# A fused vision-attention-experts kernel: another order for the last steps of its token stage

## The reference, cut to what matters

```python
h = _L0_tok_ref(x, ...)                       # (4, 256, 192)
h = jnp.concatenate([h, txt], axis=1)         # 12 tiles of 128 rows
h = h + _L0_attn_ref(_layernorm(h, axis=-1), ...)
h = h + _L0_ffn_ref(_layernorm(h, axis=-1), ...)

# in _L0_attn_ref: 12 heads of 16, hs = the normed rows
q = hs @ Wq.T + bq
v = hs @ Wv.T + bv
q = jnp.swapaxes(q.reshape(s, b, NH, HD), 0, 1).reshape(NH, BN, HD)
q = q / jnp.maximum(jnp.linalg.norm(q, axis=2, keepdims=True), 1e-12)
v = jnp.swapaxes(v.reshape(s, b, NH, HD), 0, 1).reshape(BN, NH, HD)
```

## Time and profile before

| what | value |
|---|---|
| three runs | 743.79, 733.47, 739.37 us, median 739.37 |
| the profiled execution's own time | 738.72 us |
| its span, first to last instruction | 737.0 us (1.7 us lie around it) |
| mean granted clock of TensorE | 0.94 of 2.4 GHz |
| busy, share of the span | PE 86%, DVE 58%, ACT 52%, POOL 48% |

### The profile page before, as it was taken

The page is one execution under the profiler, slowest core; times in us unless marked ns, Lnnn a source line. Parts: engine busy times, 40 slices in busy tenths (PEclk is TensorE's granted clock), DMA queues, the critical chain, the costliest instruction groups (busy, mean ns, idle before and its releaser), DMA issues.

```text
span 737.0 us, 17256 instructions
## 1 busy us (share of the span) xinstructions
PE 634.6 (86%) x4926; PEld 428.6 (58%) x4927; DVE 429.7 (58%) x1430; ACT 379.7 (52%) x721; POOL 356.2 (48%) x401
## 2 busy tenths in 40 slices
PE   5888899888884999899999998549999999999970
PEld 5775786677641223222222223438999999999970
DVE  0347767676664235555555554537777777777750
ACT  0323438343312999988999898014344344344330
POOL 3112233222232125555555545514777787787781
PEclk9999999999985999999999999559999999999995
DMA  8999999400014426545555231059898999999834
GB/s 325 409 353 303 328 313 333 164 1 1 23 53 112 68 115 192 154 143 140 150 153 150 58 71 58 37 191 300 214 249 230 229 252 235 232 255 231 228 64 77
DMA packets 78192, 132.61 MB, mean 180 GB/s; under 512 B 36859, under 2 KB 62892, under 8 KB 76876
## 3 DMA queue, kind: packets, MB, share of 16 engines
q1 hardware_dynamic: 64892, 116.79, 50.7%
q0 software_dynamic: 11712, 14.19, 11.7%
q10 hardware_dynamic: 1552, 1.18, 0.5%
HBM read 105.53 MB, written 58.42 MB: 222 GB/s over the span
## 4 chain that ended last, share of the span: by engine, by line
PE 58%; DVE 10%; ACT 9%; DMA 8%; issue 6%; POOL 6%; another core or an unknown queue 1%; SPq 1%; ACTq 0%; DVEq 0%; POOLq 0%
PE ps L864 11%; PE ps L1015 9%; PE ps L851 9%; PE ps L1044 6%; PE ps L1025 5%; DMA odd_sum<-mid 4%; ACT big L1137 3%; ACT mid L1137 3%; PE ps L701 2%; PE ps L710 2%; POOL rstd L492 2%; DVE stat L1225 1%; DVE mid L1233 1%; PE ps L786 1%; DMA out<-mid 1%
## 5 line engine op out<-in xcount | busy, mean ns | idle before, releaser
L1137 ACT ACTIVATE mid<-ps 128x1536 f32<-128x1536 f32 x108 | 152.6, 1457 | 27.1 <-PE ps L851 26.3
L627 POOL TENSOR_TENSOR mid<-mid 128x384 f32<-128x384 f32 x63 | 81.2, 1289 | 53.2 <-DVE mid L1563 23.8
L851 PE MATMUL ps<-mid 52*128 52x512 f16 x432 | 88.0, 396 | 20.7 <-ACT big L1137 8.5
L1015 PE MATMUL ps<-mid,big 128*128 128x128 f32 x756 | 99.3, 282 | 0.3 <-ACT mid L1163 0.3
L1015 PEld LDWEIGHTS ps<-mid,big 128*128 128x128 f32 x756 | 91.5, 194 | 4.6 <-ACT mid L1163 0.5
L1554 DVE TENSOR_SCALAR mid<-ps,big 128x128 f32<-128x128 f32 x189 | 54.6, 344 | 62.0 <-PE ps L1025 34.7
L864 PE MATMUL ps<-mid 128*32 128x384 f32 x864 | 87.3, 507 | 0.0
L1170 ACT ACTIVATE mid<-mid 128x384 f32<-128x384 f32 x63 | 32.9, 522 | 88.4 <-DVE mid L1554 74.6
L1044 PE MATMUL ps<-big,mid 128*128 x378 | 71.0, 332 | 4.6 <-POOL mid L627 3.9
L851 PEld LDWEIGHTS ps<-mid 52*128 52x128 f16 x432 | 17.1, 95 | 85.8 <-ACT mid L1137 46.1
L1044 PEld LDWEIGHTS ps<-big,mid 128*128 128x128 f32 x378 | 60.1, 190 | 9.8 <-issue 9.6
(11 more groups left out here) (224 smaller groups left out, 1108.6 us busy)
## 6 DMA issues: line engine op xcount, KB each, us to landing
big<-w_cat SPq DMA_DIRECT2D x63, 576.0 KB
expert_in<-expert_in SPq DMA_DIRECT2D x16, 1774.5 KB, 48.4
big<-expert_in SPq DMA_DIRECT2D x63, 136.5 KB
w_cat<-w_a SPq DMA_DIRECT2D x4, 1536.0 KB, 7.6
big<-w SPq DMA_DIRECT2D x2, 2304.0 KB, 8.9
big<-patches SPq DMA_DIRECT2D x8, 512.0 KB, 8.8
big<-patches SPq DMA_DIRECT2D x2, 2048.0 KB, 21.9
w_cat<-w_b SPq DMA_DIRECT2D x2, 1536.0 KB, 7.5
```

The source lines that it names most:

```text
L627: nc.gpsimd.tensor_tensor(actv[r], prod[r], sig[r], ALU.mult).then_inc(actv_ready, 1)
L851: last = nc.tensor.matmul(SETS[kb % 2][:, c * 512:(c + 1) * 512], keysT[n_par][row:row + STK, kb * P:(kb + 1) * P], qrysT[n_par][row:row + ...
L1015: last = nc.tensor.matmul(banks[half][:, c * P:(c + 1) * P], w1_t[q][:, half * FF + c * P:half * FF + (c + 1) * P], xtT[r][:, 0:P], start= ...
L1137: nc.scalar.activation(probs[kb % 4], SETS[kb % 2], ACT.Exp, scale=0.5).then_inc(probs_ready, 1)
```

## The change

The last 18 steps of the list are put in an order written out by hand, `CLOSE`. The order before, from the same step on, was: PP text(8,11), PT0, H1, T2, D2(3), PP0, PT1, H2, T3, S0, PP1, PT2, H3, S1, PP2, PT3, S2, PP3. ACT copies the projections instead of DVE, so PP takes banks 2 and 3. The norms get two sets of small tiles, `h_nrm` and `hnT` two pairs, and in some steps the statistics of a norm are taken in one step and the scaling (`norm_apply`, `head_norm`) is put later. POOL's five memsets of the stacks move from S0 to the PT step of text tiles (2, 5), with two more memsets and a wait. SP sends head 0's stacks before the v of images 2 and 3, with b1 and b2 right behind the stacks, and gathers the quarters of images 2 and 3 together at the end.

```diff
+CLOSE = [("PT", 0, 0), ("PP", 0, None), ("D2", 1, 3), ("H", 0, 1), ("T", LAYERS, 2), ("PP", 0, 0), ("T", LAYERS, 3),
+         ("PT", 0, 1), ("H", 0, 2), ("H", 0, 3), ("S0", 0, 0), ("PP", 0, 1), ("PT", 0, 2), ("PT", 0, 3),
+         ("S1", 0, 0), ("S2", 0, 0), ("PP", 0, 2), ("PP", 0, 3)]
...
+    begin = names.index(("PP", 0, None), names.index(("PP", 0, None)) + 1)
+    named = dict(zip(names[begin:], order[begin:]))
+    order[begin:] = [named[name] for name in CLOSE]
...
-ACC_JOBS = {"conv": 2, "A": 2, "K": 1, "C": 2, "D2": 2, "H": 2, "PP": 2}
-ACT_JOBS = {"T": 1, "A": 2, "D1": 2, "PT": 1}
+ACC_JOBS = {"conv": 2, "A": 2, "K": 1, "C": 2, "D2": 2, "H": 2}
+ACT_JOBS = {"T": 1, "A": 2, "D1": 2, "PT": 1, "PP": 2}
...
                 if stage == "S2":
                     sp.wait_ge(acc_taken, weights_read)
                     stacks(0, 0)
+                    sp.dma_start(b1_rows, w1_b[CB:CB + 1, :].rearrange("o (k c) -> (o k) c", c=P)).then_inc(b1_in, 16)
+                    sp.dma_start(b2_sb, b2).then_inc(b2_in, 16)
                 if stage == "PP":
-                    sp.wait_ge(acc_taken, jobs)
+                    sp.wait_ge(act_taken, acts)
...
-                    if b is not None:
+                    for image in {None: (), NB - 1: (NB - 2, NB - 1), NB - 2: ()}.get(b, (b,)):
 
                         sp.wait_ge(v_out, 16 * sent)
...
             sp.wait_ge(v_in, 16 * NB)
-            sp.dma_start(b1_rows, w1_b[CB:CB + 1, :].rearrange("o (k c) -> (o k) c", c=P)).then_inc(b1_in, 16)
-            sp.dma_start(b2_sb, b2).then_inc(b2_in, 16)
...
+                if stage == "PT" and tiles[0] == 2:
+
+                    pool.wait_ge(acc_taken, ctx_jobs)
                     nc.gpsimd.memset(key_both[:, :, :, 50:52], -0.5).then_inc(consts_ready, 1)
...
+                    for i, t in enumerate(hnT[1]):
+                        pool.wait_ge(consts_ready, NCONST + 5 + i)
+                        nc.gpsimd.memset(t[CB:CB + 1, P:2 * P], 1.0).then_inc(consts_ready, 1)
+                    pool.wait_ge(consts_ready, NCONST + 7)
+                if stage == "S0":
                     norm_root(0)
...
+                if stage == "PP":
+                    for t in tiles:
+                        src = act_job()
+                        nc.scalar.activation(qv[:, t, :], src[:, 0:2 * C], ACT.Identity).then_inc(act_taken, 1)
...
+            def head_norm(count, tiles):
+
+                if count >= 2:
+                    dve.wait_ge(act_ready, pt_jobs[count - 2])
+                norm_apply(head_lns[count], [h_res[:, t, :] for t in tiles], h_nrm[count % 2])
...
-                    image_norm(b)
+                    if (stage, l, b) == ("D2", LAYERS - 1, NB - 1):
+                        norm_stats2(image_rows(x_res, b))
+                        late_norm = lns[0] - 1
+                    else:
+                        image_norm(b)
...
                 if stage in ("H", "N"):
-                    if pt_job:
-                        dve.wait_ge(act_ready, pt_job)
-                    layer_norm([h_res[:, t, :] for t in tiles], h_nrm)
+                    norm_stats2([h_res[:, t, :] for t in tiles])
+                    head_lns.append(lns[0] - 1)
+                    if stage == "N" or b == 0:
+                        head_norm(len(head_lns) - 1, tiles)
+                    if (stage, b) == ("H", 1):
+                        norm_apply(late_norm, image_rows(x_res, NB - 1), image_rows(x_nrm, NB - 1))
+                    if (stage, b) == ("H", 3):
+                        head_norm(len(head_lns) - 2, rest)
+                    rest = tiles
...
                 if stage == "PT":
-                    pt_job = acts
-                if stage == "PP":
-                    for t in tiles:
-                        src = acc_job()
-                        nc.vector.tensor_copy(qv[:, t, :], src[:, 0:2 * C]).then_inc(acc_taken, 1)
+                    if b in (1, 3):
+                        head_norm(len(head_lns) - 1, tiles)
+                    pt_jobs.append(acts)
                 if stage == "S0":
-                    dve.wait_ge(acc_taken, acc[0])
+                    dve.wait_ge(act_taken, acts)
                     prep_squares(0)
```

More of the change, by code:

```diff
@@ L74, in schedule @@
     order[1:3] = [order[2], order[1]]
+    names = [job[:3] for job in order]
+    begin = names.index(("PP", 0, None), names.index(("PP", 0, None)) + 1)
+    named = dict(zip(names[begin:], order[begin:]))
+    order[begin:] = [named[name] for name in CLOSE]
     return order
 NORMS = ("conv", "C", "D2", "H", "N")
-ACC_JOBS = {"conv": 2, "A": 2, "K": 1, "C": 2, "D2": 2, "H": 2, "PP": 2}
-ACT_JOBS = {"T": 1, "A": 2, "D1": 2, "PT": 1}
-TOK_ACC = sum(ACC_JOBS.get(_s, 0) for _s, *_ in schedule())
+ACC_JOBS = {"conv": 2, "A": 2, "K": 1, "C": 2, "D2": 2, "H": 2}
+ACT_JOBS = {"T": 1, "A": 2, "D1": 2, "PT": 1, "PP": 2}
+TOK_ACC, TOK_ACT = [sum(_jobs.get(_s, 0) for _s, *_ in schedule()) for _jobs in (ACC_JOBS, ACT_JOBS)]
 def fusion_kernel(nc, patches, conv_w, cols, rows, qkv_w, out_w, ff1_w, ff2_w, head_w, txt,
@@ L157, in fusion_kernel @@
         wqvb_sb = mid[0:CB + 1, 6528:6912]
-        hnT_both = mid[:, 6912:7424].rearrange("p (s n) -> p s n", s=2)
-        hnT = [hnT_both[:, s, :] for s in range(2)]
-        h_nrm = [mid[:, 7424 + 192 * i:7616 + 192 * i] for i in range(2)]
+        hnT_both = [t.rearrange("p (s n) -> p s n", s=2) for t in (mid[:, 6912:7424], hnT_more)]
+        hnT = [[both[:, s, :] for s in range(2)] for both in hnT_both]
+        h_nrm = [[mid[:, base + 192 * i:base + 192 + 192 * i] for i in range(2)] for base in (7424, 8752)]
         rows_sb = mid[:, 7808:7808 + 5 * D]
@@ L204, in fusion_kernel @@
         nhalf = sb("nhalf", [P, NT])
[L206 to L209, removed]
+        stat, mv = [[sb(f"{name}{i}", [P, 2, n]) for i in range(2)] for name, n in (("stat", 6), ("mv", 2))]
+        vps, rstd = [[sb(f"{name}{i}", [P, 2]) for i in range(2)] for name in ("vps", "rstd")]
         sq = sb("sq", [P, C])
@@ L381, in _ @@
             v_rows = v_dram.rearrange("(t p) c -> p t c", p=P)
-            jobs = sent = 0
+            jobs = acts = sent = 0
             for stage, _, b, tiles in schedule():
                 jobs += ACC_JOBS.get(stage, 0)
+                acts += ACT_JOBS.get(stage, 0)
                 if stage == "C":
@@ L473, in _ @@
                                allow_small_or_imprecise_dtypes=True).then_inc(consts_ready, 1)
-            for i, dst in enumerate((hnT[0], hnT[1], tT)):
+            for i, dst in enumerate((*hnT[0], tT)):
                 pool.wait_ge(consts_ready, NCONST - 3 + i)
@@ L497, in norm_root @@
                 nc.gpsimd.tensor_tensor(nrm[:], ss[:], phalf[:, 0:NH], ALU.pow).then_inc(nrm_ready, 1)
-            norms, qs = 0, 0
-            for stage, l, b, _ in schedule():
-                if stage == "S0":
+            norms, qs, jobs = 0, 0, 0
+            for stage, l, b, tiles in schedule():
+                jobs += ACC_JOBS.get(stage, 0)
+                if stage == "K":
+                    ctx_jobs = jobs
+                if stage == "PT" and tiles[0] == 2:
+                    pool.wait_ge(acc_taken, ctx_jobs)
                     nc.gpsimd.memset(key_both[:, :, :, 50:52], -0.5).then_inc(consts_ready, 1)
@@ L687, in _ @@
             trks, trqs, ctxws = 0, 0, 0
-            norms, qs = 0, 0
-            norm_of, t_job, kt_of, v_job, trk_of, trq_of, ctx_job, ctxw_of, hid_job, pt_of = ({} for _ in range(10))
+            norms, qs, pts = 0, 0, 0
+            norm_of, t_job, kt_of, v_job, trk_of, trq_of, ctx_job, ctxw_of, hid_job, pt_of, half_of = ({} for _ in range(11))
             for stage, l, b, tiles in schedule():
@@ L1083, in _ @@
             act.wait_ge(cols_in, 16)
-            kts, trks, acc, half = 0, 0, 0, {}
+            kts, trks, acc, pts, half = 0, 0, 0, 0, {}
             for stage, l, b, tiles in schedule():
```

76 lines of the change are left out of this document (46 added, 30 removed).

## The result

The changed kernel takes 733.99 us in the median of 20 runs (726.14 to 741.57), the kernel before 740.74 (732.86 to 748.02, 20 runs). The ratio is 0.9909, with a 95% interval of 0.9882 to 0.9936: 6.7 us faster, between 4.7 and 8.7. That is 0.9%, less than the 2% that the prediction took for no change (it gave this 0.94), but the interval leaves out no gain. The forecast was 731.0 in 724.5 to 738.3, with 7.9 us gained.

What follows compares the result with a forecast made beforehand. It took a chain of transfers between token stage and head 0, each issued after the last landed, as the bound. Earlier stacks, SP's order and b1 off the chain bring ACT's feeding from 243.04 to 235.1: 7.9 us, 731.0, range 724.5 to 738.3.

Steps and rivals of the forecast that it cites:

- The sum: All terms up to ACT's steady feeding in head 0: 7.9 us earlier; the forecast case, chance 0.58.
- finish line: In head 0, the time from which ACT is fed block after block, 243.04 before; nothing is changed from there on.
- rival B: Stage before head 0 does not shorten; only SP's order and b1 are left: gain 5.0, 733.7, chance 0.12.
- Rival A: Head 0's v comes later: gathers in sequence (+3.2), PE wholly at 1.2 GHz (+0.7): gain 4.0, 734.7, chance 0.16.
- The first term: DVE finishes head 0's stacks, `prep(0)`, at 219.4 instead of 222.26, 2.9 us earlier.
- The moved memsets: POOL's memsets go to about 185 us: 0.44 taken back at the old place, 0.3 paid at the new one.
- Gathers: Ahead of head 0, two gathers of v, the second issued 0.35 later, 3.2 us each, landing at 230.9.
- The fall near 215: During projections of images 2 and 3, PE at half rate for 8.7 us from 214.6, as before: done at 224.8.
- SP's cover: Before head 0, SP wants image 3's projections only at 225.0, so copies ending at 220.4 or 224.8 are in time.
- SP's order: Before head 0, stacks' transfers queued behind image 2's gather hold head 0 back by 4.1 us.
- C: Clock falls in nine more heads cost 10.9 us; less 7.9 that is 3.0 slower, 741.7, chance 0.04.
- D: Clock up at head 0, 1.85 less; with PE, stores on time, memsets hidden, at most 2.7 more: 728.1, chance 0.10.

## Why the prediction was right, and where it was not

- **The sum.** 7.9 forecast, 8.6 measured at the finish line of the trace, 6.7 (4.7 to 8.7) in the whole time. The whole time by itself, 733.99, lies nearer to rival B's 733.7 and A's 734.7 than to 731.0, and the median before had moved as well, from 739.37 (3 runs) to 740.74 (20 runs). It is the trace that tells the forecast from them: ACT was fed at 234.43, where B's gain of 5.0 would have given 238.0 and A's 4.0 would have given 239.0. Its terms on the changed kernel held: stacks sent at 218.27 (219.45), first scores 223.44 (225.05), weighted products 231.04 (231.4), ACT fed 234.43 (235.1), b1 out of the chain, head 1's stacks at 230.52 ("near 231").
- **The first term was short.** The stacks were finished at 218.19 instead of 219.4. Most of it was there early: H2's sum began at 207.51, 0.8 ahead of my 208.3. The moved memsets cost what I took: the scaling beside them, at 184.70, took 0.86 where it had been 0.60, so 0.26 against 0.3.
- **Gathers.** From the issue of the first to the landing of the second it took 4.7, not 0.35 + 3.2. The stores landed 1.5 earlier than in my sum (by 225.81 against 227.35), most of it by the 1.2 of the stacks, which paid for it. That the weighted products came within 0.4 of the forecast is luck in this part: 1.5 early and 1.1 late. Rival A's mechanism existed, at a third of its price.
- **PE's side and the clock.** The fall near 215 did not come again (0.89 over 212 to 227), so image 3's copies ended at 219.35 without need of SP's cover. That step was wrong; it cost nothing, since SP came to v only at 222.64. At head 0 the clock was down as forecast for the weighted products (2.79), but full for the score block behind them, which gave 0.3.
- **The parts.** The step that failed is the sharing out of the gain. I wrote that SP's order holds head 0 back by 4.1 us, that the splits of the norms save about 1.1 each, and priced the copies by the 4.0 us that DVE loses ahead of `prep(0)`. The runs show: copies alone 8.4, SP's order alone 2.5 (about 4 without the clock's share in that profile; b1 alone 2.5), both with the old list and whole norms 8.3, the hand-written list and the split on top of these 0.3. I had treated the end of image 3's copies as something SP's queue would cover, and never asked why it was at 227.90 before: it stood behind `prep(0)` in DVE's queue, with PE held by its banks.
- **The split and the list** cancel once the copies are ACT's. The list with whole norms costs 5.3 (55.2 against 49.9), the split gives it back. In the changed kernel the squares of tile 0 come at 211.25 and DVE then waits 1.59 for their root; on the old list the squares come before H3 and the wait for the root is filled by H3. Both end at the same time, 33.2 to 33.7 after D1.
- **Rivals.** B (the stage does not shorten) did not come: the stacks were finished 4.1 earlier (218.19 against 222.26). C (slower through falls of the clock) did not come either. D (more than forecast) came for 0.7: 0.4 up to the weighted products and 0.3 by the clock. C's mechanism goes with the scatter: between the 14 profiles, whose heads run the same instructions, the heads' length differs by up to 12 us. Whether the changed kernel draws more falls than the one before is open; one or two profiles of each can't say it, and the 1.9 us between 8.6 and 6.7 is within the interval.

## What to carry to other kernels

When a copy out of PSUM stands in an in-order queue behind long work for the next stage, its price is not its own time but the whole queue ahead of it, and TensorE's banks pass it on: here copies of 0.5 us held back the end of a stage by 8. Look for products that are made long before they are taken, before working on the order of steps. And run each part of a combined edit alone: two parts here (a list and a split) only repaired each other once the copies had moved, and two others (copies and SP's order) overlapped. And look at the clock in each profile before a difference of 1 or 2 us is put down to the edit: in two runs here it made up 1.2 and 1.5 us.

## What the runs showed of the hardware

- Two small stores issued on ACT's queue beside two DMA transposes on SP's took 3.4 to 4.0 us to land, where such stores take 1.7 at the median; the transposes became 1.1 us slower.
- Of two gathers of a quarter of v issued 0.4 apart the second took 4.3 us (4.7 from the first issue), one alone 3.2.
- Two profiles of one kernel differ in how long TensorE stays at 1.2 GHz after the same waits: full clock from 233.8 in one, and in the other not before a further pair of blocks, 1.7 us more by the first head's end.
- In a stage of identical instructions, the granted clock over 190 us lay between 0.91 and 0.97, and the length between 215.5 and 203.1 us.
- VectorE's scaling of a tile pair took 1.11 us beside POOL's memsets against 0.67, and 0.86 against 0.60 at their new place.
